# The down products of two groups of expert tiles in every second step, in a macaron FFN / attention / FFN kernel

## The reference

```python
x = x + 0.5 * ffn(layernorm(x))
x = x + attention(layernorm(x))      # 16 heads of 64, causal, blocks of 256 tokens
x = x + 0.5 * ffn(layernorm(x))

def ffn(x):                          # 64 experts of width 64, the best 8 for each token
    tidx, tw = gate(x)               # sigmoid scores, 4 of 8 expert groups, then the top 8
    y = 0
    for e in range(64):
        h = silu(x @ Wg[e]) * (x @ Wu[e])
        y += w_dense[:, e, None] * (h @ Wd[e])
    return y + silu(x @ Sg) * (x @ Su) @ Sd
```

## Time and profile before

| | |
|---|---|
| median of 3 runs | 1599.59 us (1598.91 to 1600.77) |
| the profiled execution | 1599.95 us |
| its span in the trace | 1598.2 us |
| TensorE busy | 1525.0 us, 95% |
| VectorE busy | 1166.0 us, 73% |
| ScalarE busy | 766.1 us, 48% |
| GpSimd busy | 715.0 us, 45% |
| `quads` in the first FFN | 395.9 to 528.5 us |
| `quads` in the second FFN | 1201.7 to 1328.2 us |

### The profile page before, as it was taken

The page is one execution under the profiler, slowest core; times in us unless marked ns, Lnnn a source line. Parts: engine busy times, 40 slices in busy tenths (PEclk is TensorE's granted clock), DMA queues, the critical chain, the costliest instruction groups (busy, mean ns, idle before and its releaser), DMA issues. The chain is left out here.

```text
span 1598.2 us, 27345 instructions
## 1 busy us (share of the span) xinstructions
PE 1525.0 (95%) x8683; PEld 969.3 (61%) x8683; DVE 1166.0 (73%) x3354; ACT 766.1 (48%) x2105; POOL 715.0 (45%) x1093
## 2 busy tenths in 40 slices
PE   5899999999899899999999999999999999999998
PEld 2344444444788677777777776776438884444443
DVE  4698888765354578899898988764796845668675
ACT  2234323222455577777777776775325552232222
POOL 1000088888222234333333204665831226878730
PEclk9999999999999899999999999999999999999999
DMA  9999655563587101000000000112646884666552
GB/s 186 217 255 248 158 127 139 130 147 93 156 225 219 56 24 26 23 23 25 23 25 23 18 2 31 49 49 70 162 107 172 228 222 112 147 143 150 134 131 66
DMA packets 202043, 181.31 MB, mean 113 GB/s; under 512 B 39408, under 2 KB 154288, under 8 KB 201904
## 3 DMA queue, kind: packets, MB, share of 16 engines
q1 hardware_dynamic: 175056, 132.34, 35.2%
q0 software_dynamic: 16384, 33.59, 7.7%
q10 hardware_dynamic: 10464, 13.63, 2.5%
HBM read 121.83 MB, written 57.67 MB: 112 GB/s over the span
## 5 line engine op out<-in xcount | busy, mean ns | idle before, releaser
L868 ACT ACTIVATE f_hid<-banks 128x512 f32<-128x512 f32 (+1 forms) x264 | 157.6, 597 | 507.4 <-PE banks L828 507.3
L488 POOL DMA_INDIRECT x_rows<-r_xk,r_idx x256 | 262.8, 1026 | 125.8 <-issue 51.7
L890 DVE TENSOR_TENSOR f_hid<-banks,f_hid 128x512 f32<-128x512 f32 (+1 forms) x264 | 181.7, 688 | 144.2 <-ACT f_hid L868 144.0
L840 PE MATMUL banks<-f_hid,wd 128*128 128x512 f32 x528 | 272.7, 600 | 10.6 <-DVE f_hid L903 10.6
L824 PE MATMUL banks<-r_xT_d,gu 128*128 128x512 f32 x528 | 276.5, 606 | 4.2 <-DMA wd<-in_L_ffn_We_down 2.6
L828 PE MATMUL banks<-r_xT_d,gu 128*128 128x512 f32 x528 | 272.5, 598 | 0.0
L524 POOL DMA_INDIRECT a_g<-y_rows,r_idx x128 | 126.8, 990 | 237.3 <-ACT a_probT L1386 93.1
L903 DVE TENSOR_TENSOR f_hid<-f_mix_wide,f_hid 128x512 f32<-128x512 f32 x256 | 176.0, 688 | 30.3 <-DMA f_mix_wide<-mix_rows 27.9
L840 PEld LDWEIGHTS banks<-f_hid,wd 128*128 128x128 f32 x528 | 99.3, 191 | 143.4 <-issue 119.5
L828 PEld LDWEIGHTS banks<-r_xT_d,gu 128*128 128x128 f32 x528 | 101.0, 191 | 130.2 <-issue 126.4
L824 PEld LDWEIGHTS banks<-r_xT_d,gu 128*128 128x128 f32 x528 | 97.2, 192 | 119.5 <-issue 109.9
(11 more groups left out here) (243 smaller groups left out, 2875.7 us busy)
## 6 DMA issues: line engine op xcount, KB each, us to landing
f_mix_wide<-mix_rows SPq DMA_DIRECT2D x124, 512.0 KB
x_rows<-zero ACTq DMA_DIRECT2D x12, 1024.0 KB, 6.4
f1q_xq<-x_rows SPq DMA_DIRECT2D x48, 256.0 KB, 3.2
y_rows<-f1q_yq SPq DMA_DIRECT2D x48, 256.0 KB, 2.4
f2q_xq<-x_rows SPq DMA_DIRECT2D x48, 256.0 KB, 3.3
y_rows<-f2q_yq SPq DMA_DIRECT2D x48, 256.0 KB, 2.5
x_rows<-r_xk,r_idx POOLq DMA_INDIRECT x256
wd<-in_L_ffn_We_down SPq DMA_DIRECT2D x7, 512.0 KB, 10.8
```

Of the source, the lines that this page charges most:

```text
L488: nc.gpsimd.indirect_dma_start(x_rows[:, :], bass.IndirectOffsetOnAxis(ap=b.idx[:, f, CT * k + t, j:j + 1], axis=0), b.xk[:, k, t, :], Non ...
L840: mm = nc.tensor.matmul(acc[:, :], w["wd"][0:rows, 2 * p, :], d.hid[0:rows, g % HIDS, :], start=(p == 0), stop=(p == PAIRS))
L868: nc.scalar.activation(d.hid[0:rows, g % HIDS, :], gate_bank[g % 3][0:rows, :], ACT.Silu)\
L890: nc.vector.tensor_tensor(d.hid[0:rows, g % HIDS, :], up_bank[g % 3][0:rows, :], d.hid[0:rows, g % HIDS, :], ALU.mult).then_inc(gated, 1)
```

## The change

The down products of two groups now stand together. In an odd step j TensorE does `down(j-4)` and then `down(j-3)`; in an even step it does none. Group 0 (step 3) and group 51 (step 54) stand alone, the other 50 groups form 25 pairs (1,2), (3,4) ... (49,50). The even group of a pair writes the first halves of banks 5 and 6, the odd group the second halves. `down` waits for `y_read` once per pair, for everything before it; `take_y` of either group waits until both products of the pair are done, and VectorE takes the two outputs one after the other in the odd step. `hidT` gets four buffers in place of two, and `copy_hidT` waits for the product of four groups earlier. SyncE's code, GpSimd's and the order of their instructions are as before.

```diff
+HIDT_BUFS = 4
...
-    ends = banks[8].rearrange("p (s j n d) -> p s j n d", s=2, j=2, n=CT // 2)[:, :, 0]
+    halves = banks[8].rearrange("p (s j n d) -> p s j n d", s=2, j=2, n=CT // 2)
+    ends = [halves[:, :, half] for half in range(2)]
...
+    def downs_at(j):
+        if j == QUADS_ALL + 2:
+            return (j - 3,)
+        return [i for i in (j - 4, j - 3) if ok(i)] if j % 2 else ()
+
+    def down_with(j):
+        return min(j + j % 2, QUADS_ALL - 1)
...
             pe.wait_ge(hT_copied, j + 1)
-            if j >= 1:
-                pe.wait_ge(y_read, j)
+            if j % 2 or j == 0:
+                if j >= 1:
+                    pe.wait_ge(y_read, j)
...
-                mm = nc.tensor.matmul(ends[:, side, n, :], q.hidT[rows, j % 2, n, :], wt,
+                mm = nc.tensor.matmul(ends[j % 2][:, side, n, :], q.hidT[rows, j % HIDT_BUFS, n, :], wt,
...
-            if ok(j - 3):
-                down(j - 3)
+            for i in downs_at(j):
+                down(i)
...
-            if j >= 2:
-                act.wait_ge(y_done, j - 1)
+            if j >= HIDT_BUFS:
+                act.wait_ge(y_done, j - HIDT_BUFS + 1)
...
-            dve.wait_ge(y_done, j + 1)
+            dve.wait_ge(y_done, down_with(j) + 1)
+            end = ends[j % 2]
...
-            if ok(j - 3):
-                take_y(j - 3)
+            for i in downs_at(j):
+                take_y(i)
```

More of the change, by code:

```diff
@@ L667, in copy_hidT @@
             act.wait_ge(hid_turned, j + 1)
-            if j >= 2:
-                act.wait_ge(y_done, j - 1)
-            nc.scalar.copy(q.hidT[:, j % 2, :, :], C[:, 0:2 * P].rearrange("p (t n) -> p t n", n=P))\
+            if j >= HIDT_BUFS:
+                act.wait_ge(y_done, j - HIDT_BUFS + 1)
+            nc.scalar.copy(q.hidT[:, j % HIDT_BUFS, :, :], C[:, 0:2 * P].rearrange("p (t n) -> p t n", n=P))\
                 .then_inc(hT_copied, 1)
@@ L696, in take_y @@
                 for side in range(2):
-                    ins = nc.vector.scalar_tensor_tensor(x[:, side], ends[:, side], 0.5, x[:, side],
+                    ins = nc.vector.scalar_tensor_tensor(x[:, side], end[:, side], 0.5, x[:, side],
                                                          ALU.mult, ALU.add)
@@ L704, in take_y @@
             nc.vector.tensor_copy(q.yq[:, i % YBUFS, :, :].rearrange("p (n s) d -> p n s d", s=2),
-                                  ends.rearrange("p s n d -> p n s d"))\
+                                  end.rearrange("p s n d -> p n s d"))\
                 .then_inc(y_read, 1)
@@ L771, in quad_buffers @@
     q.sg, q.hid = sb("sg", [P, 2, CT * F]), sb("hidq", [P, 2, CT * F])
-    q.hidT, q.yq = sb("hidT", [P, 2, CT // 2, P]), sb("yq", [P, YBUFS, CT, D])
+    q.hidT, q.yq = sb("hidT", [P, HIDT_BUFS, CT // 2, P]), sb("yq", [P, YBUFS, CT, D])
     return q
```

## The result

| | before | after |
|---|---|---|
| median of the runs | 1600.18 us (1598.91 to 1601.82) | 1616.07 us (1612.05 to 1622.75) |
| the profiled execution | 1599.95 us | 1612.76 us |
| its span | 1598.2 us | 1611.0 us |
| routed part of the first FFN | 120.7 us | 128.4 us |
| routed part of the second FFN | 119.7 us | 125.7 us |

The changed kernel is slower: the ratio is 1.0103 [1.0071, 1.0134], four runs of each. The "routed part" runs from the first transposes of a routed group to the start of the last output copy. The spans differ by 12.8 us, and the two routed parts by 7.7 + 6.0 = 13.7; the rest of the program lies within 1.5 us of before. So everything is to be looked for in `quads`.

A forecast was written before the change was run, and what follows sets the result against it. TensorE's row of starts was taken as the bound. Edges saved, against loads, packets, stage end and VectorE, gave +0.1 us in the first FFN and -0.6 in the second: 1599.5 us, range 1589 to 1607.

The forecast's parts named there:

- edges saved: TensorE, whole to half array and back around `down`: 0.37 us saved per pair, 25 pairs, 9.2 us per FFN.
- late loads (burst and packets): SyncE's loads behind paired stores: 5.3 us bursts cost +2.8 and +1.9 us, instruction packets +6 and +4, by FFN.
- register loads ahead of `gate_up`: TensorE before `gate_up`: waits and register loads were said to show no gap there; no cost was forecast.
- end of the stage: Last groups of each FFN: a longer last link ends the stage 6.6 us after step 52's start, not 6.1: +0.5.
- VectorE's full stretch: Second FFN, some 13 steps with VectorE nearly full: 6 pairs gain nothing, +2.2 us, and load terms shrink by a third.
- Rival 2: SyncE's queue: a burst of four takes 5.75 us and makes the kernel slower, 1607 us; chance 0.28.
- Rival 1: Loads hold up, burst about 5.0 us, packets cost less, TensorE gets its gain: 1589.7 us; chance 0.33.
- Rival 3: The edges belong to each `down`, so nothing is gained and some stalls add 2 us: 1601.5 us; chance 0.05.
- the case without any cost of loads: Rival 1's variant where burst and packets cost nothing: -15.2 us, 1584.8 us.

The follow-up runs named there:

- a_lag7: Changed kernel with STORE_LAG 7 for 6, each store one place later in SyncE's queue: 1603.31 us, ratio 0.9915 to the kernel before; repeated 0.9925.
- a_split: Changed kernel with STORE_LAG 7 and the hidden transposes between the two down products of an odd step: 1620.72 us, ratio 1.0013 to the kernel before.
- after_2: The changed kernel again, unaltered, in the second group of runs: 1617.88 us, ratio 1.0101 to the kernel before.
- hoist_2: Changed kernel with the register loads of the experts' numbers moved ahead of the transposes: 1606.83 us, ratio 1.0047 to the kernel before.
- b_burst: Kernel before, without paired products, but with SyncE's loads brought in pairs, the even load held back two steps: 1731.53 us, ratio 1.082 to the kernel before.

## Why the prediction was wrong

The median lies at 1616.07 us, above the range of 1589 to 1607 and 16.6 above the forecast. Of the 14.2 us by which the profiled routed parts missed the forecast's sum, 10.6 are one term that had been set to nothing.

| term, us | predicted, FFN 1 / 2 | measured, FFN 1 / 2 |
|---|---|---|
| edges saved | -9.2 / -9.2 | -9.2 / -9.2 |
| late loads (burst and packets) | +8.8 / +5.9 | +9.8 / +8.0 |
| register loads ahead of `gate_up` | 0 / 0 | +5.9 / +4.7 |
| end of the stage | +0.5 / +0.5 | +0.9 / +1.0 |
| VectorE's full stretch | 0 / +2.2 | 0 / +1.0 |
| sum | +0.1 / -0.6 | +7.4 / +5.5 |
| the routed parts | | +7.7 / +6.0 |

The edges are counted, 25 pairs by the 0.37 us that 4.33 leaves of 4.70, and not read off as a sum. The waits are the gaps at the weight loads, summed: 9.8 for rows in the first FFN after its first wait, 8.0 in the second; 6.5 and 5.2 ahead of `gate_up`, less the 0.6 and 0.5 that `a_lag7` has as well. VectorE's term is what TensorE waited for `gated` in the second FFN beyond its end. 0.8 us are in none of these.

**The edges: right.** The clean pair took 4.33 for a predicted 4.32, and `a_split` shows that the 0.36 go with each run of half-array products and with nothing else that the pairs brought. The Trainium skill (TensorEngine Tiling (Array Packing), Key Properties) says that changing the tiling mode drains TensorE; these runs agree and price one run of half-array products at 0.36 us. The whole gain was 8.1 us in the first FFN of `a_lag7`, about the predicted 9.2 less the longer end. In its second FFN it was 4.6: the longer end and its waits for VectorE, for rows and ahead of `gate_up` are 3.5 of the difference, and 1.1 stay open.

**Burst and packets: near in the sum, wrong in the shares.** The late loads cost 9.8 us in the first FFN for a predicted 8.8, and 8.0 in the second for 5.9. The length of a burst was well taken: 5.2 to 5.8 us without a packet for 5.3. But each of 20 bursts had been expected to cost 0.14 by itself, 2.8 and 1.9 us in the two FFNs. Of the 12 bursts without a packet TensorE waited for one, 0.5 us; in `after_2` it waited for none of 15. The 28 bursts with a packet in them or just ahead go with 16.6 us of waits in the two FFNs, where 10 had been forecast. That the sum of the first FFN came near is in part luck. No run takes the packets away, so this is read off the traces alone.

The prediction also looked at one load of two. It gave a reserve for the second load of a pair only; for the first its own times, issued at T + 4.02 and due at T + 7.10, leave 3.08 us, less than the 3.2 of a single landing, and that had no term. The first load is the one waited for in 7 of 12 cases (3.7 of 9.8 us) in the first FFN and in 9 of 12 (5.9 of 8.0) in the second. One of them, with a packet that starts at 489.08:

```profile
489.11 1.59 SPq L754 DMA_DIRECT2D f1q_xq<-x_rows  x1
493.05 0.42 PEld L592 LDWEIGHTS banks<-ident,f1q_xq 128*128 128x128 f32 x4 [0.96 <-DMA f1q_xq<-x_rows]
```

Its issue alone takes 1.59 us where 0.51 is usual, and with it the second store and load come later. In the second FFN the load terms had also been shrunk by a third for VectorE's full stretch, and they weren't smaller by that; why was not tried.

**The register loads: the step that failed.** The prediction put it as: "These steps have waits and register loads before `gate_up` too and show no gap there." The steps of the earlier trace rows have no register loads at all. They belong to the shared expert, for which `load_experts` returns at once, and the first load of this kind in the kernel before starts at 408.9 us, ten after them:

```profile
L594 PEldq TENSOR_LOAD <-r_ids x96: 328/338/763, 408.9 to 1320.9; - x96
```

Steps like that of the earlier trace rows do have them and show no gap, but TensorE did not wait for rows there, and I carried this over to a kernel in which I myself forecast such waits. A register load of 0.34 us and four register operations of 0.05 make some 0.5 us that must be over before the next weights can be loaded. While the queue runs ahead of the array they are, and after a wait they are not. The gap is 0.62 behind the wait of 1.54 in the rows above, and 10.6 us in all. In the first FFN there are 18 such gaps for 12 waits in the routed groups: behind a short wait the gap is often split in two, such as 0.19 and 0.39 in two steps in a row. `hoist_2` removes it (to nothing in the list, 11 us at the median, 8.9 in the traced routed parts, since the waits for rows grow), `a_lag7` removes it by removing the waits, and `b_burst` brings it into the kernel before by adding waits. I call it shown.

**The end: right in sign, half in size.** From the last transposes to the last copy it is 8.3 us where it was 7.4. The last links of the first FFN, for the earlier trace rows:

```profile
533.14 1.29 DVE L716 COPY f1q_yq<-banks 128x512 f32<-128x512 f32 x2 [1.63 <-PE banks L647]
534.63 0.37 PE L647 MATMUL banks<-wd,f1q_hidT 64*128 x1 [1.54 <-issue]
535.39 0.69 DVE L716 COPY f1q_yq<-banks 128x512 f32<-128x512 f32 x1 [0.96 <-PE banks L647]
```

Two copies run in one go ahead of the last product, as forecast.

**The rivals.** Rival 2, slower by the loads behind the pair's stores, had the sign and the place, and 0.28 of the chance. Its price was wrong in kind: it needed a burst of 5.75 us, and what decided was not the burst but that the waits for it cost over half as much again as they last (10.6 on 17.8 us). Rival 1, the full gain, was given 0.33 on the ground that 0.1 us decides; with loads that are in time it is what happens, and `a_lag7` is at 14 us below the kernel before, where the case without any cost of loads had been put 15 below. Rival 3 is excluded by `a_split`. Pricing the register loads would have brought the forecast near: the prediction counted on some twenty loads held up by packets in the two FFNs, and 0.5 us behind each are 10 us (an estimate from these numbers), which moves the forecast to 1609.5 and the upper end of the range to 1617. The 2 x 20 short waits of its burst term would have added to that, by an amount that no run here shows.

## What to carry to other kernels

Before work is put together so that it releases two transfers at once, count the time from issue to use for each of them: for the last one against a burst and not a single landing, and for the first one as well; if there is no reserve, move the loads of the queue one place from the releases first. Here that one number turned 1.0% slower into 0.8% faster, while it does nothing for the kernel without the pairs. And an instruction that costs nothing in a full pipeline (here a register load) is only hidden by the lead of its queue: where a change brings waits, price it in full behind each of them, or move it ahead of the wait.

## What the runs showed of the hardware

- A run of half-array products between whole-array ones costs 0.36 to 0.37 us beside its products, whether it holds four or eight fp32 products; with the whole-array transposes put between the eight it is paid twice.
- A register load of 0.34 us (up to 1.05) with its register operations shows as gaps of 0.2 to 0.6 us behind a TensorE wait, and as nothing otherwise.
- Two stores and two loads of 256 KB each in alternation take 5.2 to 5.8 us from the first issue to the last landing when no instruction packet is near (up to 6.1 in `after_2`), where a single load had taken 3.2. In three bursts of the first FFN with a 16 KB instruction packet in them the last load took 5.2 to 5.6 in place of 3.7 to 4.1, for a packet that keeps one engine for 0.9 to 1.0. The Trainium skill (DMA: Bandwidth & Descriptors, Queues, rings and completion order) says that an engine takes the descriptors of a queue in order; what stands behind a held-up part on its engine then waits as well. The rows don't contradict that, and no run here isolated it.
- The issue of a load on SyncE takes 0.51 us as a rule. In the nine cases in which it took over 1.1 (up to 1.72), four before the change and five after it, an instruction packet started within 0.3 us of it.
- The kernel before takes 1600 us on one chip and 1617 on two others. The part between the two FFNs' routed parts took 680 us in its trace on the first, and 695 to 703 in the traces of the variants on the others.
